# Other order at both ends of the attention rounds, other banks and places in the experts and the routing

## The reference, cut to what matters

```
x += mlstm(layernorm(x), ctx, ctx)       # 16 heads of 32: gates (x@Wi, x@Wf), decay matrix D = exp(...),
                                         # (q k^T * D) v, divided by a normaliser, layernorm per head
x += sum_g w[t,g] * down_g(silu(gate_g x) * up_g x)   # 8 groups, w from softmax and top 8 of 32
x += long convolution of ctx*ctx products with a kernel, times layernorm(x)
x += shared(x) + sum_e routed_e(chosen tokens)        # 7 experts; each keeps the best 585 tokens
```

## Time and profile before

| | |
|---|---|
| median of 3 runs | 2050.74 us |
| profiled execution | 2051.07 us |
| its span, first to last instruction | 2049.3 us |
| TensorE busy, its mean granted clock | 1907.4 us (93%), 0.961 of full |
| VectorE busy | 1390.9 us (68%) |
| ScalarE busy | 802.3 us (39%) |
| GpSimd busy | 641.1 us (31%) |

### The profile page before, as it was taken

How to read it: one execution, slowest core, us unless ns; L and a number is a source line. 1 busy time by engine, 2 the same in 40 slices (tenths; PEclk the granted TensorE clock), 3 DMA queues, 4 the chain that set the end, 5 groups by cost and what they waited for, 6 DMA issues and landing times. The chain is left out here.

```text
span 2049.3 us, 35178 instructions
## 1 busy us (share of the span) xinstructions
PE 1907.4 (93%) x13798; PEld 1624.9 (79%) x13798; DVE 1390.9 (68%) x2817; ACT 802.3 (39%) x1484; POOL 641.1 (31%) x507
## 2 busy tenths in 40 slices
PE   4799999999999999999999996999898989988997
PEld 2578888888888888999999995777676788767886
DVE  5678788888888866655555553678866857784554
ACT  4545555555554533222221221445444443232332
POOL 2433334333333331000000000677655720003553
PEclk7799999999999999999999998999999977999999
DMA  4212211111121123322222223535533444224774
GB/s 132 81 58 73 83 70 67 63 63 63 63 83 63 73 73 124 114 85 101 103 94 98 98 73 147 178 108 158 155 108 126 151 145 146 99 107 145 178 177 63
DMA packets 111751, 214.66 MB, mean 105 GB/s; under 512 B 14242, under 2 KB 34786, under 8 KB 110562
## 3 DMA queue, kind: packets, MB, share of 16 engines
q1 hardware_dynamic: 104194, 195.30, 28.2%
q0 software_dynamic: 7392, 17.11, 4.1%
HBM read 136.11 MB, written 76.34 MB: 104 GB/s over the span
## 5 line engine op out<-in xcount | busy, mean ns | idle before, releaser
L1400 PE MATMUL psum<-kv,toep 128*128 128x288 f32 x1280 | 326.0, 417 | 43.7 <-ACT yx L1448 26.5
L1400 PEld LDWEIGHTS psum<-kv,toep 128*128 128x128 f32 x1280 | 247.9, 195 | 119.2 <-ACT yx L1448 32.1
L168 PE MATMUL psum<-xn_t_h,w_gate_h 128*128 128x256 f32 x768 | 232.8, 303 | 1.3 <-DVE xn_th L293 1.3
L168 PE MATMUL psum<-xn_t_h,w_up_h 128*128 128x256 f32 x768 | 217.3, 283 | 0.0
L169 PE MATMUL psum<-xn_t_l,w_up_h 128*128 128x256 f32 x768 | 217.3, 283 | 0.0
L170 PE MATMUL psum<-xn_t_h,w_gate_l 128*128 128x256 f32 x768 | 217.2, 283 | 0.0
L169 PE MATMUL psum<-xn_t_l,w_gate_h 128*128 128x256 f32 x768 | 217.2, 283 | 0.0
L170 PE MATMUL psum<-xn_t_h,w_up_l 128*128 128x256 f32 x768 | 216.6, 282 | 0.0
L1062 POOL TENSOR_SCALAR_AFFINE_SELECT operands<-operands 128x512 f32<-128x512 f32 x128 | 95.1, 743 | 333.6 <-ACT operands L805 333.4
L161 POOL TENSOR_TENSOR rstd<-rstd,minus_half 128x2 f32<-128x2 f32 x48 | 35.2, 733 | 518.2 <-DVE rstd L157 518.2
L276 ACT ACTIVATE xn_th<-psum 128x256 f32<-128x256 f32 x192 | 73.8, 384 | 309.5 <-PE psum L170 308.4
(11 more groups left out here) (311 smaller groups left out, 4804.8 us busy)
## 6 DMA issues: line engine op xcount, KB each, us to landing
toep<-ssm_padded_scratch SPq DMA_DIRECT2D x64, 256.0 KB, 3.5
kx<-in_ctx_pairs SPq DMA_DIRECT2D x32, 384.0 KB, 4.4
x_scratch<-x_all SPq DMA_DIRECT2D x21, 512.0 KB, 2.8
x_all<-in_x SPq DMA_DIRECT2D x16, 512.0 KB, 3.8
operands<-in_ctx_t SPq DMA_DIRECT2D x16, 512.0 KB, 4.8
xn_t_scratch<-xn_t_h SPq DMA_DIRECT2D x16, 512.0 KB, 2.7
xn_t_scratch<-xn_t_l SPq DMA_DIRECT2D x16, 512.0 KB, 3.6
xn_t_h<-xn_t_scratch SPq DMA_DIRECT2D x16, 512.0 KB, 3.6
```

Of the source, the lines that this page charges most:

```text
L168: pe.run.matmul(out, lhs[0], rhs[0], start=first, stop=False)
L1400: ins = pe.run.matmul(out, w[:, (o - k) * P:(o - k + 1) * P], pairs, start=(k == 0), stop=(k == o))
```

## The change

It reorders `first_operands`, `first_slots`, rounds 16 and 17 of `slots`, and the last slot of round 15. `gates` is cut in two: `gate_keys` (the eight products with the context) and the rest; for rounds 0 to 2 `gate_keys` has its own place. `weights` is cut into `weights_high` (ACT) and `weights_low` (DVE). The last two `weights2` go into the second pass. Some turns get other banks. In the last layer the output list takes one more link between its second and third output, a count ahead of parts 0 and 4 is moved ahead of `product`, some links are left empty, four of the five first slot turns move ahead of the last `hidden_low`, and the routed outputs use banks 6, 7, 2, 3, 6.

```diff
+                first_operands = [("load_rest", 0), ("load_values", 0), ("load_x", 1), ("load_weights", 0), ("load_ctx", 1),
+                                  ("load_weights", 1), ("load_x", 2), ("normalise_x", 0), ("apply_x", 0), ("turn_query", 0, 0),
+                                  ("turn_query", 0, 1), ("setup", 0), ("gate_keys", 0), ("sum_values", 0), ("gates", 0),
+                                  ("setup_router", 0), ("gate_keys", 1), ("gates_log", 0), ("normalise_x", 1),
+                                  ("weights_high", 0), ("apply_x", 1), ("decays", 0), ("turn_query", 1, 0), ("parts", 0),
+                                  ("norms", 0), ("rows", 0), ("turn_query", 1, 1), ("values", 0), ("weights_low", 0),
+                                  ("load_weights", 2), ("weights_high", 1), ("weights_low", 1), ("load_weights", 3)]
                 first_slots = [
+                    [("step", 0, 0), ("exp", 0, 0), ("gates", 1), ("load_values", 1), ("store_kernel", 0)],
                     [("step", 0, 1), ("exp", 0, 1), ("gates_log", 1)],
+                    [("step", 0, 2), ("exp", 0, 2), ("decays", 1)],
+                    [("step", 0, 3), ("exp", 0, 3), ("weighted", 0, 0), ("parts", 1), ("sum_values", 1), ("weights_high", 2)],
+                    [("step", 0, 4), ("exp", 0, 4), ("turn_h", 0, 0), ("rows", 1), ("norms", 1), ("values", 1),
+                     ("weights_low", 2), ("load_weights", 4)],
+                    [("step", 0, 5), ("exp", 0, 5), ("weighted", 0, 1), ("normalise_x", 2), ("weights_high", 3)],
+                    [("step", 0, 6), ("exp", 0, 6), ("turn_h", 0, 1), ("apply_x", 2), ("weights_low", 3), ("load_weights", 5)],
+                    [("step", 0, 7), ("exp", 0, 7), ("weighted", 0, 2), ("weights_high", 4)],
+                    [("step", 0, 8), ("turn_h", 0, 2), ("weights_low", 4), ("load_ctx", 2)],
+                    [("step", 1, 0), ("exp", 1, 0), ("weighted", 0, 3), ("turn_query", 2, 0)],
+                    [("turn_h", 0, 3), ("step", 1, 1), ("exp", 1, 1), ("sums", 0), ("turn_query", 2, 1)],
+                    [("step", 1, 2), ("exp", 1, 2), ("spread", 0, 0), ("gate_keys", 2), ("weights_high", 5), ("weights_low", 5)],
+                    [("step", 1, 3), ("exp", 1, 3), ("weighted", 1, 0), ("spread", 0, 1), ("load_values", 2), ("gates", 2)],
+                    [("step", 1, 4), ("exp", 1, 4), ("turn_h", 1, 0), ("residual", 0), ("gates_log", 2)],
+                    [("step", 1, 5), ("exp", 1, 5), ("weighted", 1, 1), ("statistics", 0), ("decays", 2)],
                     [("step", 1, 6), ("exp", 1, 6), ("normalise", 0), ("turn_h", 1, 1), ("sum_values", 2), ("parts", 2)],
+                    [("step", 1, 7), ("exp", 1, 7), ("turn_x", 0, 0), ("turn_x", 0, 1), ("weighted", 1, 2), ("rows", 2),
+                     ("norms", 2), ("values", 2)],
+                    [("step", 1, 8), ("router", 0), ("turn_h", 1, 2), ("logits", 0), ("gate_up", 0, 0), ("shares", 0)],
                     [("weighted", 1, 3)]]
...
                     if b > B:
-                        yield [("shares", f), ("gate_up", f, 0)]
-                        yield [("gate_up", f, 1), ("turn_shares", f), ("share", f, 0), ("gate_low", f, 0), ("share", f, 1)]
+                        yield [("gate_up", f, 0), ("turn_shares", f)]
+                        yield [("gate_up", f, 1), ("share", f, 0), ("gate_low", f, 0), ("share", f, 1)]
+                    elif b == B:
+                        yield [("turn_h", e, 3), ("sums", e), ("turn_shares", f)]
+                        yield [("gate_up", f, 1), ("share", f, 0), ("gate_low", f, 0), ("spread", e, 0), ("share", f, 1)]
...
                     if b >= B:
-                        yield [("gate_up", f, 5), ("share", f, 5), ("gate_low", f, 5), ("normalise", e), ("down", f, 0),
-                               ("turn_x", e, 0), ("turn_x", e, 1), ("down", f, 1), ("store_x2", f), ("router", e), ("logits", e)]
+                        yield [("gate_up", f, 5), ("share", f, 5), ("normalise", e), ("gate_low", f, 5), ("turn_x", e, 0),
+                               ("turn_x", e, 1), ("down", f, 0), ("router", e), ("logits", e), ("shares", e), ("down", f, 1),
+                               ("store_x2", f)]
                         return
...
-                    yield [("weighted", a, 3)]
+                    yield ([("gate_up", e, 0)] if b == B - 1 else []) + [("weighted", a, 3)]
...
-                        banks.plan((name, b, at[0]), 5 if b in (1, 2) else 6)
+                        banks.plan((name, b, at[0]), ((6, 5), (5, 4), (5, 5))[b][at[0]] if b < 3 else 6)
...
+                    for jl in range(1, 3):
+                        order2.append(("gate_up", b, jl))
+                        if b == 0 and jl <= JH // PER:
+                            order2.append(("weights2", GH + jl - 1))
...
-            links += [([], [])] * 6 + [([], [("score_turn",)])]
+            links += [([], [])] * 6 + [([], [("score_turn",)]), ([], [])]
             links += [([("count", i)], [("total", i)]) for i in range(len(BITS))]
-            links += [([("final",)], [("final_total",)]), ([("choose",)], [("place",)]), ([("number",)], [("slots_turn",)]),
-                      ([("slots",)], [])]
+            links += [([("final",)], [("final_total",)]), ([("choose",)], []), ([], [("place",)]),
+                      ([("number",)], [("slots_turn",)]), ([("slots",)], []), ([], [])]
             for c in range(2 * TOKT // HOT):
                 links.append(([("hot", c)], [("table", c - 1)] if c else []))
+                if c in (2, 5):
+                    links.append(([], []))
...
                     order.append(("hidden", blk, f, half_, piece))
                     order += after_part
+                    before_part, after_part = next(links, ([], []))
+                    if part % 4 == 3 and before_part and before_part[0][0] == "count":
+                        order += before_part
+                        before_part = []
+                    if blk == NBLK - 1 and part in (4, 5, 6):
+                        order.append(("slot_turn", 0, part - 4))
                     if part % 4 == 3:
                         order.append(("product", blk, f))
                     if part == 1 and blk:
                         for j in range(BLK):
+                            if j == 2:
+                                order += before_part
                             order.append(("out", blk - 1, j))
+                            if j == 2:
+                                order += after_part
+                                before_part, after_part = next(links, ([], []))
...
-            order.append(("hidden_low", NBLK - 1, 1))
-            order += [("slot_turn", 0, i) for i in range(NT)]
+            order += [("slot_turn", 0, 3), ("hidden_low", NBLK - 1, 1), ("slot_turn", 0, 4)]
...
-                    banks.plan((name, *at), 6 + at[1] % 2)
+                    banks.plan((name, *at), (6, 7, 2, 3, 6)[at[1]])
```

More of the change, by code:

```diff
@@ L492, in build_program @@
                 first_slots = [
-                    [("step", 0, 0), ("exp", 0, 0), ("gates", 1), ("load_values", 1), ("store_kernel", 0), ("weights", 0),
-                     ("load_weights", 2)],
+                    [("step", 0, 0), ("exp", 0, 0), ("gates", 1), ("load_values", 1), ("store_kernel", 0)],
                     [("step", 0, 1), ("exp", 0, 1), ("gates_log", 1)],
-                    [("step", 0, 2), ("exp", 0, 2), ("decays", 1), ("weights", 1), ("load_weights", 3)],
-                    [("step", 0, 3), ("exp", 0, 3), ("weighted", 0, 0), ("parts", 1), ("sum_values", 1)],
@@ L504, in build_program @@
-                    [("weighted", 0, 3)],
-                    [("step", 1, 0), ("exp", 1, 0), ("turn_h", 0, 3), ("sums", 0), ("turn_query", 2, 0)],
-                    [("step", 1, 1), ("exp", 1, 1), ("turn_query", 2, 1), ("spread", 0, 0), ("weights", 4)],
-                    [("step", 1, 2), ("exp", 1, 2), ("spread", 0, 1), ("load_values", 2), ("gates", 2)],
-                    [("step", 1, 3), ("exp", 1, 3), ("weighted", 1, 0), ("residual", 0)],
-                    [("step", 1, 4), ("exp", 1, 4), ("turn_h", 1, 0), ("statistics", 0), ("gates_log", 2)],
@@ L588, in head_rows, with second_high, second_low @@
                     return slice(h % 4 * DH, (h % 4 + 1) * DH)
+                pieces2 = dict(weight_pieces(1, stages2))
+                def second_high(piece):
+                    key = ("gate_up", B - 1, 0, JH - 1) if piece < GH else ("down", B - 1, 0, ST - 1)
+                    bank, filled, emptied, n = banks.at(*key)
+                    act.wait_ge(filled, n + 1)
+                    act.wait_ge(stage2_loaded[piece], loaded_by(piece, len(stages2)))
+                    for src, parts_ in pieces2[piece]:
+                        act.run.copy(parts_[0], src).then_inc(weight_high, 1)
+                def second_low(piece):
+                    dve.wait_ge(stage2_loaded[piece], loaded_by(piece, len(stages2)))
```

(20 more changed lines are left out.)

59 lines of the change are left out of this document (24 added, 35 removed).

## The result

The changed kernel takes 2043.6 us in the median of 16 runs (2039.36 to 2050.28), the kernel before, on the same chip, 2053.14 (2047.85 to 2057.94, 16 runs). The ratio of the two, taken side by side, is 0.9961, its 95% interval 0.9952 to 0.9969: 8.0 us, 0.39% faster. The forecast was 2041 with 2031 to 2050, and "faster" with 0.71.

The account below looks back on a forecast made before the run. TensorE's waits at the start, last rounds, routing and routed experts were taken to reach the program's end. 2051.07 - 8.5 (start) + 5.8 (last rounds) - 0.1 (routing) - 7.0 (experts) = 2041.3, 2041.0 against the median; range 2031 to 2050.

Parts of the forecast that it names:

- (d): Routing, to the last block's outputs: the chain ends earlier and the hot tables' waits shrink; 1.9 us won.
- (e): Routing, slot turns between the last block's parts: waits merge into one of 2.7; 1.6 us won, 1.6 more if clock holds.
- First two rounds: Start of the kernel: reordered products, splits and loads bring step (2,1) 8.5 us earlier; bounds 5 and 12.1.
- Rival B: The start gives only 4 us, as half-clock steps fill what the earlier order frees; 2045.5 us; chance 0.10.
- Last two rounds: Waits for the share's bank and before the turn of x, plus half clock: net 5.8 us lost; bounds 2 won, 9 lost.
- (a): Routing: score's copy and first count move behind two output products, a 2.5 us wait becomes 1.6; 0.9 won.
- (c): Routing: the extra count among output products delays `out_add` 1, so `out` 3 waits for its bank; 1.3 us lost.
- (b): Routing: counts at parts 0 or 4 ahead of `product` lose 1.13 us six times against 0.37 before; 4.6 lost.
- Experts: Routed experts: new output banks remove six waits of 1.17 with nothing behind them; 7.0 us won, bounds 4 and 7.
- Rival C: Routed experts: bank change only moves the wait, the next expert waits the 1.17; 2048 us; chance 0.07.
- Rival A: Last rounds and counts do not stall; 5.8 and 4.6 us mostly come back, about 2033; chance 0.2.
- D: Rival, counting blocks: many short stalls take the clock down, 3.4 us a fall; six make 2062; chance 0.08.

Follow-up runs that it names:

- e3: The changed kernel with rounds 16 and 17 and the end of round 15 in the old order: 2039.20 us, 0.9935 of the kernel before.
- e4: The changed kernel with only `down` (14,0) put back ahead of `turn_x` 15: 2045.03 us, 0.9963 of the kernel before.
- e9: The changed kernel, unchanged, timed again on a third chip: 2051.67 us, 0.9979 of the kernel before.
- e2: The changed kernel with counts at parts 0 and 4 back behind `product`: 2039.95 us, 0.9944 of the kernel before.
- e5: The changed kernel with rounds 16 and 17 and all routing links as before: 2038.19 us, 0.9910 of the kernel before.
- e1: The kernel before with only the routed outputs' banks changed to 6, 7, 2, 3, 6: 2042.32 us, 0.9958 of the kernel before.

## Why the prediction was right, and where it was not

The sum came within 3 us because errors of both signs met. The leads above add up to 6.1 us for a forecast of 9.8: the start and the experts won 2.35 us more than forecast; `(d)`, `(e)`, the routing's first half and the convolution lost 5.8 more, the last rounds 0.2. Step by step:

- **First two rounds**, 8.5 forecast for step (2,1), 10.9 measured, of which 9.35 last to `down` (13,1). Steps (0,0) and (0,2) came as forecast, at 27.90 (28.1) and 34.71 (34.5), and the lead at step (1,3) was 13.15 (12.1). Then two errors met. At step (1,7) the lead was 6.6 for 8.8: "late next is VectorE" was right, but the term was too small, with waits of 3.0 and 2.9 us for VectorE's product before steps (1,6) and (1,7) and `residual` at 3.25 us of VectorE for 2.5. From there to step (2,1) 4.2 us were won where 0.3 lost were forecast, although the 2.79 us of waiting for the shares had been put at 1.3: `gate_up` (0,0) ran at full clock. The walk priced work at half clock and had no term for that, so the good match at the end is in part luck. Rival B, 4 us, is refuted.
- **Last two rounds**, 5.8 lost forecast, 6.0 measured, and e3 gives 7.2 back with the weight pieces left where they are. The mechanisms are those predicted: 1.78 for about 2 in round 16, 4.26 for 4.5, the 0.86 gone. That the same wait in round 15's experts would grow from 0.90 to 1.78 was not forecast. The 2.5 for the clock was right in size and wrong in place: it fell to 0.66 behind the first 1.78 (the `gate_up` behind it takes 4.6 us, the next one 3.1) and to 0.88 behind the 4.26. That `down` (14,0) alone was the cover is refuted by e4: `gate_low` ahead of `normalise` belonged to it.
- **Routing (a) to (c)**, 5.0 lost forecast, 5.9 measured from the first turn behind the convolution to block 4's outputs, and 5.5 in e4 and e9. How it divides at block 0's first output depends on the clock. In after 2.1 were won up to there, for 0.9, with the clock at 0.82 for 0.70, and 8.0 lost behind it, for 5.9, with the clock at 0.72 for the first 6.2 us; e4 and e9 lose 6.5 there. The term of (b), 4.6, was right in idle time: the waits on a total are 5.9 in after and 1.3 in e2. (c) was put at 1.3, with waits at the third output; no wait on `out_add`'s banks appears in the counting blocks, and what remained in e2 is 1.6 over three blocks.
- **(d)**, 1.9 won forecast, 0.15 measured. The waits for the hot tables fell from 4.0 to 1.3 as said, but waits on `out_add`'s banks, 3.8 us in three, stand in their place (1.4 in one in before and in e5, which has the old links): I had counted `slots` and the two hots against the chain, not against the outputs.
- **(e)**, 3.2 forecast, 1.95 measured. Its first half was added up wrongly: 2.5 and 1.1 less 2.7 is 0.9, not 1.6. The wait came as said (3.05 for 2.7); the clock did not recover, the outputs still took 7.2 us for 7.3 before.
- **Experts**, 7.0 forecast, 8.5 measured (8.3 in e1). An expert takes 22.1 us for 23.5, 1.4 for each wait of 1.17. Rival C is refuted.
- **The convolution** took 1.9 more, which no edit explains and which lies within what e1 shows between two runs of one code.

Rival A fails: the last rounds and the counts did stall. So does D: with six waits of 0.9 to 1.3 us the clock was 0.98 from 1724 to 1795, and what is missing to 1 fell in the first 6.2 us, ahead of all six. The rule of the Trainium skill that spoke for it ("TensorE: Matmul & The Clock Gate", section "A second HAM failure mode: psum-queue depth-cycling") is not borne out at such waits in these blocks, where TensorE is otherwise dense.

## What to carry to other kernels

A product moved ahead of the stage it waits for needs a look at what had covered the wait, on both engines: the cover was `down` on TensorE and `gate_low` on VectorE, and putting back one of them gave a third of the gain. A short serial chain threaded through a pipeline was best placed in the gap that the other engine leaves (the count between `pr` and `hidden_l`), and cost 4 to 5.5 us ahead of it. And where many edits are timed as one, measure them by stages: here one line of bank numbers was worth the whole, and the good edits (banks, start) were paying for the bad ones (last rounds, counts).

## What was not expected of the hardware

- The same wait of 1.78 us, at the same place of two successive rounds, was followed by a clock of 0.66 over five microseconds the first time and of 1.00 the second; the same wait of 4.26 by 0.88 in one kernel and 0.51 in another. The length of an idle alone does not tell what the clock does. Nor does the code alone: behind block 0's first output the same code ran at 0.72 in after and at 1.00 in e4.
- At the first `gate_up` the clock was 0.96 to 1.00 in eight traces of one and the same start, 0.79 in a ninth, and 0.66 and 0.60 in the two with a part of the start put back. Arriving sooner does not decide it: the one with 0.79 had arrived 1.0 us before after. A difference of some 2 us there in a single trace says nothing about an edit.
- ScalarE and VectorE stood still for up to 5.4 us around the time in which GpSimd issues its gathers, in one place of the program, in all eight profiles of two chips and in none of the six others, and the profile names no releaser.
